# A graph layer on one core: scaling and most of the first-pass copies move to GpSimd, and the far rows' slots become tile slots at the end

## The reference

```python
def _L0_gnn_ref(x, adj, w):                     # x 8192x128, adj 8192x8192, w 128x128, fp32
    A = adj + jnp.eye(adj.shape[0], dtype=adj.dtype)
    deg = jnp.sum(A, axis=1)
    d_isqrt = jax.lax.rsqrt(deg)
    A_hat = A * d_isqrt[:, None] * d_isqrt[None, :]
    h = jnp.matmul(A_hat, x)
    return jax.nn.elu(jnp.matmul(h, w))
x = _layernorm(x + _L0_gnn_ref(x, adj, L0_gnn_w), axis=-1)
```

## Time and profile before

| | |
|---|---|
| time, median of 3 runs | 1083.79 us (1083.71 to 1086.43) |
| the profiled execution: its own time | 1086.72 us |
| the profiled execution: span | 1084.9 us |
| PE busy | 929.3 us |
| DVE busy | 832.0 us |
| ACT busy | 759.0 us |
| POOL busy | 53.6 us |
| DMA read from HBM | 359.20 MB |

### The profile page before, as it was taken

The page is one execution under the profiler, slowest core; times in us unless marked ns, Lnnn a source line. Parts: engine busy times, 40 slices in busy tenths (PEclk is TensorE's granted clock), DMA queues, the critical chain, the costliest instruction groups (busy, mean ns, idle before and its releaser), DMA issues.

```text
span 1084.9 us, 35847 instructions
## 1 busy us (share of the span) xinstructions
PE 929.3 (86%) x16128; PEld 851.6 (79%) x16128; DVE 832.0 (77%) x770; ACT 759.0 (70%) x1777; POOL 53.6 (5%) x55
## 2 busy tenths in 40 slices
PE   0079399597796999989999999999999999999994
PEld 0065289597796989878989799789988999888894
DVE  0487587686877787878889799999899876756963
ACT  6898898898988989897997989882152867200202
POOL 0000000000000000000000000010001000000000
PEclk9999789899898999989999999999999999999997
DMA  9999999999999999999998999896977987888960
GB/s 380 400 391 411 396 400 403 394 399 392 398 397 386 390 371 393 366 388 352 387 383 325 349 390 317 292 315 215 312 251 240 328 281 248 273 286 263 356 245 21
DMA packets 168841, 365.72 MB, mean 337 GB/s; under 512 B 6256, under 2 KB 34032, under 8 KB 160496
## 3 DMA queue, kind: packets, MB, share of 16 engines
q1 hardware_dynamic: 151792, 355.03, 89.6%
q10 hardware_dynamic: 16896, 8.39, 2.7%
HBM read 359.20 MB, written 4.19 MB: 335 GB/s over the span
## 4 chain that ended last, share of the span: by engine, by line
PE 59%; DMA 16%; DVE 11%; ACT 7%; issue 4%; SPq 2%; POOL 0%; DVEq 0%; ACTq 0%
PE p_set L858 58%; DMA space<-in_adj 15%; ACT space L764 5%; DVE space L876 5%; DVE space L896 2%; SPq L723 2%; DVE hT L907 1%; DVE xn L889 1%; ACT space L772 1%; PE p_set L836 1%; DMA xn<-in_x 1%; DVE stats L936 1%; DVE space L930 0%; ACT space L795 0%; POOL d L748 0%
## 5 line engine op out<-in xcount | busy, mean ns | idle before, releaser
L858 PE MATMUL p_set<-space 32*128 32x256 f32 (+3 forms) x16000 | 912.5, 385 | 141.1 <-DVE space L876 88.1
L858 PEld LDWEIGHTS p_set<-space 32*128 32x128 f32 x16000 | 836.2, 188 | 213.6 <-issue 146.2
L876 DVE STREAM_TRANSPOSE space<-space 128x2048 f32<-128x2048 f32 x256 | 580.1, 2292 | 113.0 <-ACT space L764 64.3
L764 ACT ACTIVATE space<-space 128x512 f32<-128x512 f32 (+2 forms) x744 | 577.8, 778 | 70.1 <-DMA space<-in_adj 66.2
L907 DVE TENSOR_TENSOR hT<-p_set,hT 128x1024 f32<-128x1024 f32 (+2 forms) x100 | 106.3, 1077 | 81.7 <-PE p_set L858 81.3
L772 ACT ACTIVATE space<-xn 32x512 f32<-32x512 f32 x192 | 120.3, 627 | 45.7 <-DVE xn L889 36.8
L764 ACT ACTIVATION_READ_ACCUMULATOR space<-space 128x1 f32 x744 | 138.8, 187 | 0.0
L787 ACT ACTIVATE space<-space 128x512 f32<-128x512 f32 x16 | 10.1, 629 | 172.5 <-DVE space L918 172.4
L896 DVE COPY space<-xn 32x512 f32<-32x512 f32 x160 | 66.8, 417 | 5.0
L748 POOL TENSOR_TENSOR d<-deg,half 128x4 f32<-128x4 f32 x16 | 16.3, 1018 | 699.4 <-DVE deg L882 699.4
L795 ACT ACTIVATE space<-space,shift,rstd 128x128 f32<-128x128 f32 x64 | 26.2, 481 | 27.5 <-DVE shift L951 27.4
(11 more groups left out here) (14 smaller groups left out, 17.5 us busy)
## 6 DMA issues: line engine op xcount, KB each, us to landing
space<-in_adj SPq DMA_DIRECT2D x324, 1024.0 KB, 12.3
space<-in_adj SPq DMA_DIRECT2D x12, 768.0 KB, 12.3
xn<-in_x SPq DMA_DIRECT2D x22, 256.0 KB, 9.4
space<-in_x ACTq DMA_DIRECT2D x16, 256.0 KB, 7.4
out_rows<-space ACTq DMA_DIRECT2D x16, 256.0 KB, 7.3
w_sb<-in_w SPq DMA_DIRECT2D x1, 64.0 KB, 1.9
```

Of the source, the lines that this page charges most:

```text
L764: ins = nc.scalar.activation(view[:, g], view[:, g], ACT.Copy, accum_out=to[:, g:g + 1])
L858: ins = nc.tensor.matmul(to, xs_chunk(h, j)[quadrant(q)], moving, start=first and s == b == 0, stop=last and s == b == 3)
L876: nc.vector.transpose(slots[slot], slots[slot]).then_inc(tile_turned, 1)
```

## The change

POOL takes the scaling of x for all homes, and in the first pass the twelve copies of s = 1, 2 and 3; DVE keeps the four of s = 0 and ACT makes none there. POOL waits after each of its copies for that copy's own semaphore. In the last pass ACT still makes all sixteen. `close_stage()` is also called when the last row band's loads are all issued, so that the four stage slots are released: the first three released slots become the output stage, the others serve tiles. `KEEP` goes from (12, 11, 7) to (12, 9, 7): 55 tiles are kept and 81 come again. `STAY` 11 lets band 11 keep its home, which leaves 21 homes. Near tiles are loaded in groups of two, none of four. `FEED` goes from 12 to 10.

```diff
--- before.py
+++ after.py
@@ -13,19 +13,18 @@
 SLOTS = 22
 STAGE = 4
 LATE = 3
-KEEP = (12, 11, 7)
+KEEP = (12, 9, 7)
 AHEAD = 2
-STAY = 12
-WIDTHS = (4, 2)
+STAY = 11
+WIDTHS = (2,)
 XN = 2
 RING = 4
 SETS = 2
 MERGE = 4
-FEED = 12
+FEED = 10
 FLIGHT = 5
 EPS = 1e-5
-FIRST_COPIES = [("dve", [(0, q) for q in range(Q)]), ("act", [(2, 2), (2, 3)] + [(3, q) for q in range(Q)]),
-                ("dve", [(1, q) for q in range(Q)] + [(2, 0), (2, 1)])]
+FIRST_COPIES = [("dve", [(0, q) for q in range(Q)]), ("pool", [(s, q) for s in (1, 2, 3) for q in range(Q)])]
 LATE_COPIES = [("act", [(s, q) for q in range(Q)]) for s in range(Q)]
 
 
@@ -149,7 +148,7 @@
         order["sp"].append(("x", home_of[t]))
         dma = max(dma, now + 1.0) + XLOAD
         if t in known:
-            offer("dve", 5, "scale", home_of[t], 0.7)
+            offer("pool", 3, "scale", home_of[t], 1.35)
         return True
 
     def drop_home(t):
@@ -264,6 +263,7 @@
                     row_todo = strip_items(at_row, kept)
                 else:
                     rows_done = True
+                    close_stage()
 
     def close_stage():
 
@@ -312,7 +312,7 @@
             offer("pool", 0, "power", arg, 1.2)
         elif kind == "power":
             known.add(arg)
-            offer("dve", 0, "scale", home_of[arg], 0.7)
+            offer("pool", 0, "scale", home_of[arg], 1.35)
             if arg in held_diagonals:
                 offer("pool", 1, "diagonal", held_diagonals.pop(arg), 1.4)
         elif kind == "scale":
@@ -320,7 +320,7 @@
             copies_left[arg] = len(some)
             usable[arg] = False
             for i, (e, pairs) in enumerate(some):
-                offer(e, 0 if some is FIRST_COPIES else 4, "copies", (arg, i), (0.43 if e == "dve" else 0.64) * len(pairs))
+                offer(e, 0 if some is FIRST_COPIES else 4, "copies", (arg, i), {"dve": 0.43, "act": 0.64, "pool": 0.8}[e] * len(pairs))
         elif kind == "copies":
             h = arg[0]
             copies_left[h] -= 1
@@ -501,18 +501,18 @@
 
     sum_nth, turn_nth, diagonal_nth = nth_of("act", "sum"), nth_of("dve", "turn"), nth_of("pool", "diagonal")
     row_nth, power_nth = nth_of("dve", "row_sum"), nth_of("pool", "power")
-    scale_nth, z_nth = nth_of("dve", "scale"), nth_of("dve", "z")
+    scale_nth, z_nth = nth_of("pool", "scale"), nth_of("dve", "z")
     part_of = {i: n for n, p in enumerate(parts) for i in p[2]}
     last_part = {h: max(n for n, p in enumerate(parts) if p[1] == h) for h in range(len(homes))}
     job_end = {p[0]: n for n, p in enumerate(parts) if p[4]}
 
-    copied, copies_by = {}, {"dve": 0, "act": 0}
+    copied, copies_by = {}, {"dve": 0, "act": 0, "pool": 0}
     copied_last = {h: {} for h in range(len(homes))}
 
     def copies_of(h):
         return LATE_COPIES if any(t == homes[h][0] for t, _ in homes[:h]) else FIRST_COPIES
 
-    for engine in ("dve", "act"):
+    for engine in copies_by:
         for kind, arg in order[engine]:
             if kind == "copies":
                 h, some = arg
@@ -610,7 +610,7 @@
         row_summed = sem("row_summed")
         d_ready = sem("d_ready")
         x_scaled = sem("x_scaled")
-        copied_by = {"dve": sem("copied_by_dve"), "act": sem("copied_by_act")}
+        copied_by = {"dve": sem("copied_by_dve"), "act": sem("copied_by_act"), "pool": sem("copied_by_pool")}
         part_out = sem("part_out")
         product_added = sem("product_added")
         hw_out = sem("hw_out")
@@ -746,6 +746,20 @@
                     r = arg
                     pool.wait_ge(row_summed, row_nth[r])
                     nc.gpsimd.tensor_tensor(d[:, r], deg[:, r % 2], half[:, :], ALU.pow).then_inc(d_ready, 1)
+                elif kind == "scale":
+                    h = arg
+                    t = homes[h][0]
+                    pool.wait_ge(d_ready, power_nth[t])
+                    pool.wait_ge(x_loaded[h % XN], 16 * (h // XN + 1))
+                    nc.gpsimd.tensor_tensor(xn[:, h % XN], xn[:, h % XN], d[:, t].unsqueeze(2).to_broadcast([128, BLOCKS, F]), ALU.mult)\
+                      .then_inc(x_scaled, 1)
+                elif kind == "copies":
+                    h, some = arg
+                    pool.wait_ge(x_scaled, scale_nth[h])
+                    wait_vacant(pool, ("home", h))
+                    for s, q in copies_of(h)[some][1]:
+                        nc.gpsimd.tensor_copy(xs_part(h, q, s), xn[quadrant(s), h % XN]).then_inc(copied_by["pool"], 1)
+                        pool.wait_ge(copied_by["pool"], copied[h, (s, q)][1])
                 else:
                     n = arg
                     pool.wait_ge(var_ready, n + 1)
@@ -881,13 +895,6 @@
                         dve.wait_ge(d_ready, row_nth[r] - 2)
                     nc.vector.tensor_reduce(deg[:, r % 2], sums[:, BLOCKS * r:BLOCKS * (r + 1)], AX.X, ALU.add)\
                       .then_inc(row_summed, 1)
-                elif kind == "scale":
-                    h = arg
-                    t = homes[h][0]
-                    dve.wait_ge(d_ready, power_nth[t])
-                    dve.wait_ge(x_loaded[h % XN], 16 * (h // XN + 1))
-                    nc.vector.tensor_tensor(xn[:, h % XN], xn[:, h % XN], d[:, t].unsqueeze(2).to_broadcast([128, BLOCKS, F]), ALU.mult)\
-                      .then_inc(x_scaled, 1)
                 elif kind == "copies":
                     h, some = arg
                     dve.wait_ge(x_scaled, scale_nth[h])
```

## The result

The changed kernel takes 1069.3 us against 1083.8 before, 0.986 of it (95% interval 0.983 to 0.989). It is faster, as forecast, but by 14.5 us and not by 6.8: twice the forecast, inside the range.

The account below looks back on a forecast made before the run. PE, busy 929.3 of 1084.9 us, was taken to bound the kernel, leaving its idle time to win. Tail -9.3, middle -4.0, copies +6.3 sum to -7.0 us: forecast 1077 us, range 1060 to 1097.

Parts of the forecast that it names:

- The tail: Last pass: nine slots instead of five serve tiles, loads start earlier, and PE wins 9.3 us of idle time.
- Relief of ACT and DVE in the middle: First pass, 378 to 702 us: fewer copies and scalings on ACT and DVE win 4.0 of 16.0 us idle.
- POOL's copies: First pass, band starts: twelve copies at 1.07 us each with the gap, plus slower scaling, cost 6.3 us.
- the prediction's own formula: Cost of a band start in the first pass: 12c - 6.5 us, with c the time for a POOL copy.
- once: Band starts: the 6.3 us disappear up to 378 us, then are paid one time, not five, if loads keep their times.
- Rival D: Band starts from 343.9 to about 600 us: delay handed on through PE's slots and loads, 1096 us; 22 in 100.
- threshold of 4.2 us: Band starts: the cost of each from which rival D decides, a copy of 0.89 us with its gap.
- others go first: POOL's queue: the identity's add, up to 13 us later, is one of ten or more tiles, so others precede it.
- costs nothing: Last pass: four more tiles moved there by KEEP fit in the DMA's free room; without it, 10.6 us.
- The last sign: Prediction is wrong if the new order (FEED, groups of two) changes the times at which bands become known.
- Two engines and one port: DVE and POOL copies taking turns on shared ports make a band start cost 8.0 us instead of 6.3.
- rival B: First-pass copies: DVE and POOL block each other, adding 1.7 us, for 1079 us; 10 in 100.

Follow-up runs that it names:

- b_close_params: The changed kernel without the move to POOL: stage slots released, four constants new, copies and scaling on DVE and ACT; 1082.4 us, 0.999 of before.
- m_short: Kernel before, own queue order, scaling and twelve copies moved to POOL, copies shortened to 4 of 128 columns; 1080.4 us, 0.996 of before.
- a_short: The changed kernel with 180 of the 192 first-pass POOL copies cut to 4 of 128 columns; 1068.7 us, 0.985 of before.
- a_twice: The changed kernel with each first-pass copy on POOL made twice; 1147.6 us, 1.058 of before.
- b_moved: The kernel before, its queue order kept, with only the scaling and twelve first-pass copies moved to POOL; 1106.0 us, 1.018 of before.
- a_keep11: The changed kernel with KEEP = (12, 11, 7) as before, 59 tiles kept and 77 loaded again; 1111.9 us, 1.023 of before.

## Why the prediction was wrong

The step that failed is the price of the move to POOL: 6.3 us of copies less 4.0 of relief, a loss of 2.3. With the released slots and the new constants in both kernels the move gains 14 us (0.999 to 0.986). The other parts were forecast to gain 9.3 and gain about 1 together (b_close_params), for `KEEP` and the other constants weren't free. These two errors, 16 and 8 us, pull in opposite directions and leave 8: that the time stayed inside the range is partly luck.

**The tail** (9.3 us) was right, in place and size: 10 to 12 us. The loop of load, turn and part opened, though the 2.0 us forecast between 702 and 918 us weren't there: the win lies behind 918. One reading was off by little: up to 1072.6 us the last window had 2.2 us idle and not 2.6.

**Relief of ACT and DVE in the middle** (4.0) was about right where it could be measured alone: 5 us in m_short. What it missed is the largest piece. I looked for it between 378 and 702 us; in the new plan it is just behind, where DVE's copies of two homes stood ahead of an add (9.67 us). The rows of before showed no such wait, since there the late bands lay farther apart in time (10.0 us and not 6.7).

**POOL's copies** (6.3, paid once) is the term that failed, with its size and with the rule for how often it is paid. The size: a copy takes 0.642 us with 0.05 between two, not 0.87 with 0.2; by the prediction's own formula that is 12 x 0.69 - 6.5 = 1.8 us for a band start, and a_short finds next to nothing in the whole kernel. With that in place of 6.3 the sum would have been about 12 us and the forecast 1072; it would have come near, with the terms still wrong as above. The formula also has PE ask for a new s every 1.78 us, its full rate. At the start of band 5 the first quarter took 3.8 us at a granted clock of 0.61, which gave the copies 2 us more.

The rule: "once" can't be told from "never" in the changed kernel, and fails in the others. The cost isn't a number of the copies but of the slack around them: next to nothing in the changed kernel, 25 us for 4.7 us of each home's copies in the old order, 78 for a second set. Nor did the delay disappear up to 378 us, where I had put it at nothing: a_twice is 11 us behind at band 4, which becomes known at 350 us.

Rival D, which I gave 22 in 100, was right that a delay can come back at every band. Its threshold of 4.2 us for a start was not reached here, yet b_moved, with copies as short as the changed kernel's, lost 20 us: the threshold was wrong as a rule. Its path through the slots is not shown. In a_twice most of the idle time is PE's direct wait for copies, and in a_keep11 most of the loss has another origin.

**The identity's add** "others go first" was wrong for a fixed order: in b_moved each turn of the diagonal tile was DVE's next instruction (85.5 us of waits, 10 us of time). The plan that knows POOL's costs puts it later, and the changed kernel has no such wait.

**`KEEP`** "costs nothing" was wrong: it is what makes the move pay, 41 us between 1.023 and 0.986. I had counted its slots (three) only as a small gain. Without POOL the four constants together cost 7. The last sign that I had named for a wrong prediction did show: the new order changes when the bands become known, by 10 us at band 9 (594.9 to 585.1). It does so without POOL too: 585.7 in b_close_params.

**Two engines and one port**: right in kind, and more visible than in the rows of before. DVE is busy 784.5 us and not about 770; 16 of these are the longer copies. The rule of the Trainium skill, "SBUF — State Buffer", section "Who interferes with whom", asks for whole instructions to wait on one another. This trace agrees with the direction (0.413 us alone, 0.670 beside POOL; POOL 0.607 against 0.642) and not with the size. At band 5 DVE's four copies took 3.11 us, in which POOL was busy for 2.86, as it was in the first 3.11 us of its copies with DVE out of the way; one after the other, DVE's 4 x 0.413 and the 2.86 would be 4.5 us. DVE's four end 1.0 us later, not 4.3, and POOL's twelve take 8.32 us against 7.96 with DVE's out of the way, 0.4 more and not 1.7. So rival B's price was too high, and keeping the two apart is no cure: holding POOL back until DVE is done costs 5.

The Trainium skill's page "GPSIMD Engine Reference", section 3.1, has 769 ns for 512 elements in a tight loop. The trace's copy of 512 elements a partition took 0.612 us in the median, so the figure of that loop is 26% high for this instruction; it was nearer than my 0.87.

## What to carry to other kernels

When a loop runs load, use, free, load, ask of each delay not what it costs but whether the resource it holds is the one that the next round waits for: 4.5 us less of copies at each home gained 1.5 us in one order with 55 tiles kept, and 4.7 less gained 25 in another with 59. Work that moves to a slower engine takes with it everything behind it in that engine's queue, and in a static order the engine that waits for the last of these stands still. Price a group of edits that share a plan together, two by two if you can: here one part gained 14 us or cost 36, as another part was set.

## What the runs showed of the hardware

A short idle stretch costs PE more than its own length. In the kernel before, PE stood still from 937.5 to 939.5 us, and the next part took 8.92 us instead of the usual 7.2:

```profile
937.50:939.40 1.90, 0.00 (x0) 0.00 (x0) 1.90 (x3) 0.00 (x0) 0.80 (x1) 1.00 1.12 331
939.40:940.00 0.60, 0.52 (x8) 0.51 (x12) 0.60 (x3) 0.50 (x2) 0.00 (x0) 1.00 0.88 211
940.60:941.20 0.60, 0.60 (x16) 0.57 (x12) 0.60 (x1) 0.55 (x2) 0.00 (x0) 0.71 0.93 304
942.00:943.00 1.00, 1.00 (x12) 0.86 (x12) 0.00 (x0) 0.00 (x0) 0.00 (x0) 0.50 1.06 367
```

The granted clock is the column behind POOL's. It is still 1.00 when PE starts again, and falls only then: 0.71 from 940.6 us, 0.50 from 941.2 to 944, then back. 0.50 is the lower of its two levels, 1.2 GHz. So a wait of 2 us cost 1.7 us more behind it, which the profile counts as busy.

b_moved has the parts of the kernel before (16128 matmul records in both) and lost 20 us to it. Of these, 8.4 us are in PE's busy time, 937.7 us against 929.3, and only 11.4 are idle time; how much of the 8.4 is the clock and how much short waits inside a part, the profile doesn't separate.
